# The opening of a relative-position attention: tokens of one batch normalised first, relative scores of two jobs in sets of four strips

## The chip, the cores and the metric

The kernel runs as one program on one core of a Trainium2 chip. The metric is the device time of one execution in microseconds (us), lower is better. Inside the core, TensorE (PE in the profile; its weight loads are PEld), VectorE (DVE), ScalarE (ACT), GpSimd (POOL) and the queue of SyncE (SP), which issues most DMAs, run side by side, each in its own written order, and meet only in semaphores.

## The reference

The model is four blocks on 4 batches of 512 tokens with 256 features: an attention with relative positions, an encoder layer with a mixture of experts, a cross attention, and a second mixture of experts. Only the beginning of the first block matters here. Cut to that:

```python
def _layernorm(x, axis=-1, eps=1e-05):
    m = jnp.mean(x, axis=axis, keepdims=True)
    v = jnp.var(x, axis=axis, keepdims=True)
    return (x - m) / jnp.sqrt(v + eps)
...
q = (jnp.einsum('bsd,ed->bse', query, Wq) + bq).reshape(B, S, H, dh).transpose(0, 2, 1, 3)
k = (jnp.einsum('bsd,ed->bse', key, Wk) + bk).reshape(B, S, H, dh).transpose(0, 2, 1, 3)
v = (jnp.einsum('bsd,ed->bse', value, Wv) + bv).reshape(B, S, H, dh).transpose(0, 2, 1, 3)
QEr = jnp.einsum('bhsd,ld->bhsl', q, Er_s)
Srel = _skew(QEr)
QK = jnp.einsum('bhsd,bhtd->bhst', q, k)
attn = (QK + Srel) / math.sqrt(dh)
attn = jnp.where(causal[None, None], attn, -jnp.inf)
attn = jax.nn.softmax(attn, axis=-1)
out = jnp.einsum('bhst,bhtd->bhsd', attn, v)
...
x = x + _L0_xattn_ref(_layernorm(x, axis=-1), ctx_1024, ctx_1024, ...)
```

The query is the normalised x, key and value are the context, there are 16 heads of 16 features, and everything is f32.

## The kernel before

**Tiles and jobs.** The 2048 tokens are 16 blocks of 128 (`TB`), four to a batch (`RT`). The first attention is done in 16 jobs (`NJ`), each four heads (`HQ`) of one batch. A job has eight units (`NUA`): row block r = 0 to 3 of the batch, and in each the pairs of heads pr = 0 and 1. Because of the causal mask row block r has 128(r+1) columns. A head occupies a strip of 32 partitions, so that four heads fill the 128 rows of the PE array. Two jobs share one projection of queries (`QPa`) or keys (`Ka`), and the zero-padded tables `ErP[0]` and `ErP[1]` pick which of the two jobs' heads a relative score is of.

**The relative scores** (QEr) make a trip through DRAM, which does the skew. `scores_a` on PE multiplies `QPa` by `ErP` into the two PSUM banks of `PD[0]`, `rel_copy` on ACT copies them to `EN[r]`, `rel_write` on SP writes `EN[r]` to DRAM once both pairs are in it, `rel_read` reads it back skewed into `SR[r]`, and GpSimd masks the diagonal (`rel_mask`). The relative scores run two jobs ahead of the key scores: in unit u of loop step n `scores_a(n, u)` issues the pair of relative scores of job n+2 and the pair of key scores of job n. The steps n = -2 and n = -1 are therefore the opening: they hold the relative scores of jobs 0 and 1 and no key scores, and between them the projections `queries_a`, `keys_a` and `values_to_bank_a`. A pair of relative scores may be issued only when ACT has copied the pair before, since there is one `PD[0]`. From n = 0 on DVE adds `SR` to the key scores and takes the row maximum (`row_max_a`), ACT takes the exponential, PE transposes, ACT and DVE copy the transposed weights to `PTa`, and PE multiplies them by the values.

**What stands ahead of the steps.** SP issues the loads in the order x (2 MB, whole), identity, constants, Wq, Wk, eight small pieces of Er, the context (2 MB), Wv, three rows. DVE waits for all of x, then takes the statistics of 16 blocks (`ln_part`, L1270 and L1273), ACT the square root (L1047), DVE normalises the 16 blocks into the four buffers of `nrm` (L1281), PE transposes them through two PSUM banks (`ln_transposes`, L604) and ACT copies them to `NT` (L1054). Only when all 16 are in `NT` does PE begin the first `queries_a`.

**The shared bank.** Queries, keys, values and outputs go through one PSUM bank `MB` in the order of the table `A_USES`; a use may be written only when the use before it has been read (`a_mr`).

Of the kernel before, what the change touches and what calls it, by code (L numbers as in the profile page):

```python
# [13 lines left out]
P = 128  # L14
D = 256
DK = D // P
# [55 lines left out]
A_USES = []  # L72
for _n in range(-3, NJ + 1):
    A_USES += [("k", (_n + 1) // 2)] * (_n % 2 == 1 and 0 <= _n + 1 < NJ)
    A_USES += [("q", 0)] * (_n == -3) + [("q", (_n + 4) // 2)] * (_n % 2 == 0 and _n + 4 < NJ)
    A_USES += [("v", _t) for _t in (range(RT) if _n == -1 else [_n + RT] * (0 <= _n < TB - RT))]
    A_USES += [("p", _n - 1), ("o", _n - 1)] * (_n >= 1)
# [40 lines left out]
def build(nc, A, out):  # L118

    with ExitStack() as ctx:  # L120
# [12 lines left out]
        def place(name, shape, dt, o=None):  # L133
            n = 1
            for s in shape[1:]:
# [137 lines left out]
              ("ctx0", "w0", "const", "x", "er", "wf", "wvo", "rows0", "late", "route", "ew", "w1", "ctx1", "rows1", "we0", "we")}  # L273
# [12 lines left out]
        for name, n in [("ln0", TB), ("ln1", TB), ("kvf", NJ // 2 + TB),  # L286
                        ("ont", TB), ("wo", TB), ("ln2", TB), ("rt0", 1), ("rank", 1), ("gt", 4), ("ln3", TB), ("ln4", TB), ("rt1", 1)]:
            USE[name], N_USE[name] = n_use, n
            n_use += n
# [36 lines left out]
        a_en = sem("a_rel_copied")  # L326
        a_w = [[sem(f"a_rel_written{i}_{r}") for r in range(RT)] for i in range(2)]
# [68 lines left out]
        def _(sp):  # L396
            sp.dma_start(X[:], A["x"].rearrange("(t p) d -> p t d", p=P)).then_inc(ld["x"], 16)
            sp.dma_start(idf[:], A["ident"]).then_inc(ld["const"], 16)
            sp.dma_start(cols[:], A["cols"]).then_inc(ld["const"], 16)
            for wa, w in ((WAq, "wq0T"), (WAk, "wk0T")):  # L400
                sp.dma_start(wa[:], A[w].rearrange("(k p) n -> p k n", p=P)).then_inc(ld["w0"], 16)
# [10 lines left out]
            def rel_write(n, r):  # L412
                sp.wait_ge(a_en, n * NUA + 2 * r + 2)
                if n >= 3:
                    sp.wait_ge(a_r[r], 16 * (n - 2))
                sp.dma_start(rel[n % 3][r], EN[r][:].rearrange("p h w -> p (h w)")).then_inc(a_w[n % 2][r], 16)
# [9 lines left out]
            for n in range(-2, NJ - 1):  # L426
                for r in range(RT):
                    if n + 2 < NJ:
                        rel_write(n + 2, r)
                    if n >= -1:  # L430
                        rel_read(n + 1, r)
# [158 lines left out]
        def _(pe):  # L590
# [17 lines left out]
            ln_transposes(0, "ln0", lambda tb: nrm[:, tb % 4])  # L608
            wait_all_stored(pe, "ln0")
            pe.wait_ge(ld["w0"], 32)  # L610
            pe.wait_ge(ld["er"], 32 * HQ)
            pe.wait_ge(ld["ctx0"], 32)

# [5 lines left out]
            def eight_heads(w, k, half):  # L619

                return w[:, k, half * P:half * P + P]

# [14 lines left out]
            def scores_a(n, u):  # L637
                r, pr = divmod(u, 2)
                w, e, ku = P * r + P, n + 2, n * NSU + 2 * u
                if e < NJ:  # L640
                    if u == 0:
                        pe.wait_ge(a_mr, A_AT["q", e // 2] + 1)
                    if e * NUA + u:
                        pe.wait_ge(a_en, e * NUA + u)
# [50 lines left out]

            queries_a(0)
            for n in range(-2, NJ + 1):
                for u in range(NUA):
# [11 lines left out]
                    if u == 2:  # L710
                        for tb in range(RT) if n == -1 else [n + RT] * (0 <= n < TB - RT):
                            values_to_bank_a(tb)
# [329 lines left out]
        def _(act):  # L1042
# [18 lines left out]
            ln_part(0, "ln0")  # L1061
            act.wait_ge(s_bp, 3)
# [13 lines left out]
            def rel_copy(n, u):  # L1076
                r, pr = divmod(u, 2)
                act.wait_ge(a_e, n * NUA + u + 1)
                if n and pr == 0:
                    act.wait_ge(a_w[(n - 1) % 2][r], 16 * ((n - 1) // 2 + 1))  # L1080
# [10 lines left out]
            def weights_a(t):  # L1091
                n, u = divmod(t, NUA)
                r, pr = divmod(u, 2)
                for i in range(A_UPTO[t - 1] if t else 0, A_UPTO[t]):
                    _, js, who, _ = A_GROUPS[i]
                    if who == "act":
                        act.wait_ge(a_tr, i + 1)
                        if n >= 2:
# [10 lines left out]

            queries_a(0)  # L1110
            for n in range(-2, NJ + 1):
                for u in range(NUA):
# [11 lines left out]
                    if 0 <= n < NJ:  # L1124
# [591 lines left out]
```

## Time and profile before

| | us |
|---|---|
| median of 3 runs | 2118.84 |
| lowest and highest | 2114.27, 2118.95 |
| the profiled execution | 2133.6 |
| its span, first to last instruction | 2131.9 |
| mean granted TensorE clock, share of full | 0.913 |
| busy PE, DVE, ACT, POOL | 1822.3, 1122.8, 843.2, 204.8 |
| before the first transpose on PE | 20.34 |
| from there to the first key score of job 0 | 65.51 |
| the 16 jobs of the first attention, up to the last transposes of outputs | 293 |

The stretch that the change touches is the first 86 us of the span. After it comes the loop over the jobs, and after that the other three blocks, which begin with a wait for everything that this attention adds to x. The granted clock is that of TensorE; a share of 1.00 is 2.4 GHz, 0.50 is 1.2 GHz. A row of a timeline gives start and length in us, engine, line, operation, output and input with their shapes and how many instructions are merged in it; in square brackets stands the idle time before it and what ended it. A matmul of f32 is counted twice in these rows, so "x4" is two matmuls.

### The profile page before, as it was taken

What the parts mean: (1) busy time and instruction counts of PE and PEld (TensorE: products, weight loads), DVE (VectorE), ACT (ScalarE), POOL (GpSimd) and SP (SyncE); (2) the same over time, 40 slices, a digit from 0 to 9 for tenths busy, and PEclk for the clock granted to TensorE, in tenths of its full rate; (3) what the DMA queues carried; (4) which work ended last, traced back from release to release, by engine and by line L of the source; (5) the groups of instructions that cost most, each with busy time, mean ns of one, the idle gap of its engine ahead of it and who ended that gap; (6) DMA issues with size and microseconds to landing.
All of it is one profiled execution on the core that took longest, in us unless ns stands there. A gap on an engine that the chain in (4) does not pass through costs nothing.

```text
span 2131.9 us, 31428 instructions
## 1 busy us (share of the span) xinstructions
PE 1822.3 (85%) x10594; PEld 1061.4 (50%) x10595; DVE 1122.8 (53%) x3014; ACT 843.2 (40%) x1951; POOL 204.8 (10%) x282
## 2 busy tenths in 40 slices
PE   4799999587777863999999089999999999977998
PEld 2355555242333452676676044445455445446886
DVE  2277777634555343222222466666666666655775
ACT  2488887414444330433333044544444444430000
POOL 0011111201111305000000520000000000020000
PEclk9799999677999955999999579999999999986999
DMA  4578886300000542111110600000000000020001
GB/s 137 199 276 292 283 293 213 119 0 1 1 1 1 182 138 86 32 32 32 34 32 25 212 1 1 1 1 1 1 1 1 1 1 1 1 79 0 0 0 40
DMA packets 63691, 146.68 MB, mean 69 GB/s; under 512 B 6345, under 2 KB 41297, under 8 KB 58961
## 3 DMA queue, kind: packets, MB, share of 16 engines
q1 hardware_dynamic: 60496, 136.69, 18.9%
q0 software_dynamic: 3072, 8.39, 1.2%
q8 instruction: 73, 1.20, 0.2%
q14 instruction: 50, 0.40, 0.1%
HBM read 86.34 MB, written 58.72 MB: 68 GB/s over the span
## 4 chain that ended last, share of the span: by engine, by line
PE 78%; DVE 7%; issue 7%; ACT 6%; POOL 2%; DMA 1%; SPq 0%; DVEq 0%; ACTq 0%; POOLq 0%
PE PS L596 11%; PE PS L1036 8%; PE PS L887 7%; PE PS L875 7%; PE PS L965 5%; PE PS L975 5%; PE PS L988 5%; PE PS L653 5%; PE PS L757 5%; PE PS L675 3%; PE PS L944 3%; PE PS L953 3%; PE PS L775 2%; PE PS L686 2%; PE PS L901 2%
## 5 line engine op out<-in xcount | busy, mean ns | idle before, releaser
L1224 ACT ACTIVATE P<-PS,nm 128x512 f32<-128x512 f32 x256 | 173.5, 682 | 317.2 <-DVE nm L1561 317.2
L1561 DVE TENSOR_REDUCE nm<-PS 128x2 f32<-128x1024 f32 x128 | 156.7, 1225 | 110.8 <-PE PS L965 110.7
L1383 DVE CUSTOM_DVE_ANT_0 dump<-PS,maskw 128x256 f32<-128x256 f32 (+3 forms) x256 | 115.4, 488 | 125.8 <-PE PS L762 117.7
L1321 DVE CUSTOM_DVE_ANT_0 SN<-PS,SR 128x128 f32<-128x128 f32 (+3 forms) x256 | 115.3, 488 | 91.1 <-PE PS L657 90.8
L975 PEld LDWEIGHTS PS<-idf,P 128*128 128x128 f32 x1024 | 109.6, 141 | 106.2 <-issue 105.5
L757 PE MATMUL PS<-QP,KP 32*128 32x256 f32 (+3 forms) x512 | 112.3, 518 | 57.2 <-DVE MX L1383 42.3
L887 PE MATMUL PS<-EW,xT 128*128 x320 | 147.1, 603 | 1.8 <-ACT xT L1187 1.3
L875 PE MATMUL PS<-EW,hT 128*128 x640 | 146.5, 383 | 2.4 <-ACT hT L1199 2.4
L975 PE MATMUL PS<-idf,P 128*128 128x128 f32 x1024 | 139.3, 279 | 8.2 <-ACT PTb L1233 8.2
L965 PE MATMUL PS<-K,Q 64*128 64x512 f32 x512 | 145.5, 645 | 0.9 <-DVE Q L1549 0.9
L653 PE MATMUL PS<-ErP,QPa 32*128 32x512 f32 (+3 forms) x512 | 114.0, 520 | 29.6 <-ACT EN L1082 20.6
L1652 DVE SCALAR_TENSOR_TENSOR X<-PS,gat,X 128x256 f32<-128x256 f32 x256 | 110.9, 479 | 53.1 <-PE PS L1036 51.9
L988 PE MATMUL PS<-PTb,V 128*64 128x512 f32 x512 | 137.4, 617 | 0.8 <-ACT O1T L1248 0.8
L1152 ACT ACTIVATE PTf<-PS 128x1024 f32<-128x1024 f32 (+3 forms) x128 | 89.5, 703 | 118.1 <-PE PS L757 118.0
L1199 ACT ACTIVATE hT<-PS,b1c 128x128 f32<-128x128 f32 x320 | 86.9, 383 | 122.9 <-PE PS L901 119.8
L604 PE MATMUL PS<-idf,nrm 128*128 128x128 f32 x128 | 40.1, 439 | 108.7 <-DVE nrm L1281 103.8
L1521 DVE COPY hS<-PS 128x512 f32<-128x512 f32 x80 | 55.3, 691 | 145.6 <-PE PS L887 145.6
L1089 ACT ACTIVATE SN<-SN,nm 128x128 f32<-128x128 f32 (+3 forms) x256 | 128.7, 555 | 6.0 <-DVE nm L1321 6.0
L875 PEld LDWEIGHTS PS<-EW,hT 128*128 128x128 f32 x640 | 119.7, 192 | 18.1 <-issue 3.1
L762 PE MATMUL PS<-KP,QP 32*128 32x384 f32 (+3 forms) x512 | 121.0, 550 | 7.6 <-DVE MX L1383 6.0
L1570 DVE TENSOR_SCALAR P<-P,rc 128x512 f32<-128x512 f32 x256 | 113.0, 484 | 4.6
L1082 ACT ACTIVATE EN<-PS 128x256 f32<-128x256 f32 (+3 forms) x128 | 89.7, 701 | 50.8 <-PE PS L653 50.6
(205 smaller groups left out, 3070.9 us busy)
## 6 DMA issues: line engine op xcount, KB each, us to landing
rel<-EN SPq DMA_DIRECT2D x16, 1024.0 KB, 4.8
SR<-rel SPq DMA_DIRECT2D x16, 1024.0 KB, 7.5
rel<-EN SPq DMA_DIRECT2D x16, 768.0 KB, 4.3
SR<-rel SPq DMA_DIRECT2D x16, 768.0 KB, 6.5
rel<-EN SPq DMA_DIRECT2D x16, 512.0 KB, 2.9
SR<-rel SPq DMA_DIRECT2D x16, 512.0 KB, 5.1
EW<-in_fc1T SPq DMA_DIRECT2D x8, 1024.0 KB, 12.0
EW<-in_fc2T SPq DMA_DIRECT2D x8, 1024.0 KB, 11.7
```

The lines of the kernel that those rows point to most:

```text
L596: last = mm(bank[0:m, 0:n], w(k), src(k), start=(k == 0), stop=(k == DK - 1))
L653: rel_mm = mm(PD[0][:, i, 0:w], QPa[e // 2 % 3][o:o + HQ8, r * P:r * P + P], ErP[e % 2][o:o + HQ8, S - w:S], start=True, stop=True)
L757: keys_mm = mm(PD[s % 2][:, x, 0:S - c * P], KP[o:o + HQ8, hg, b * S + c * P:b * S + c * P + P], QP[n % 4][o:o + HQ8, c * P:S], start=True ...
L875: last = mm(PS[5][:, 0:D], hT[:, f, :], EW[:, bass.ds(e, 1), o:o + D].rearrange("p e d -> p (e d)"), start=(f == 0), stop=(f == FK - 1))
L887: ins = mm(PS[1 + hf][:], xT[:, k, :], EW[:, bass.ds(e, 1), o:o + 512].rearrange("p e f -> p (e f)"), start=(k == 0), stop=(k == DK - 1))
L965: last = mm(PD[s % 2][:, j, :], Q1[m % 2][o:o + DH1, r * P:r * P + P], K1[m % 2][o:o + DH1, :], start=True, stop=True)
L975: last = nc.tensor.transpose(TR1[j][:, c * P:c * P + P], P1[s % 4][:, j, c * P:c * P + P], idf[:])
L988: last = mm(OUT1[o:o + DH1, :], V1[m % 2][:, c, o:o + DH1], PT1[m % 2][:, j, c, :], start=(c == 0), stop=(c == RT - 1), skip_group_check=True)
L1036: last = mm(PS[tb % 8][:], x[:, k, t], w[i][:, k, :], start=(n + k == 0), stop=(n + k == len(parts) + DK - 2))
L1089: af(sn, sn, ACT.Exp, bias=nm[:, (ku + i) % 16:(ku + i) % 16 + 1], scale=-1.0).then_inc(a_ex, 1)
L1224: last = af(P1[s % 4][:, j, :], PD[s % 2][:, j, :], ACT.Exp, bias=nm1[:, s % 4, j:j + 1], accum_out=sm1[:, s % 4, j:j + 1])
L1561: v.tensor_reduce(nm1[:, s % 4, :], PD[s % 2][:], AX.X, ALU.max, negate=True).then_inc(c_max, 1)
```

## The change

It rewrites the opening on all engines and leaves the loop from job 0 on nearly alone.

- **Loads.** x comes in two pieces, the 4 blocks of the first batch (512 KB) first, and the other 12 (1.5 MB) behind the context. Wk is issued behind Er, Wv behind the second piece of x.
- **Layer norm.** Statistics, square root and normalisation are done for blocks 0 to 3 first and for blocks 4 to 15 when their piece has come. The transposes go two blocks at a time through the shared bank `MB` (`tokens_a(i)`, uses `("l", i)`), with one ACT copy of 512 columns for two blocks: 0 and 1 ahead of the first queries, 2 and 3 ahead of the loop, 4 to 7 in units 3 to 6 of step n = 0.
- **Relative scores of jobs 0 and 1.** `rel_scores_a(n, r)` issues all four strips of a row block at once, into two of three bank pairs in turn (`PD[(2 * q + pr) % 3]`, q = 4n + r), and ACT and DVE copy one pair each (`rel_copy_first`), counted by `a_en` and by the new `a_end`. Job 1 is copied to `PTa[1]` in place of `EN`.
- **Order.** Queries 0, job 0, keys 0, queries 1, job 1, the values of the first batch, and then the loop from n = 0.

```diff
 A_USES = []
-for _n in range(-3, NJ + 1):
+A_USES = [("l", 0), ("l", 1), ("q", 0), ("k", 0), ("q", 1)] + [("v", _t) for _t in range(RT)] + [("l", 2), ("l", 3)]
+for _n in range(NJ + 1):
...
+    A_USES += [("l", _i) for _i in range(4, TB // 2)] * (_n == 0)
...
+            sp.dma_start(X[:, 0:RT], tokens[:, 0:RT]).then_inc(ld["x0"], 16)
...
+            sp.dma_start(WAk[:], A["wk0T"].rearrange("(k p) n -> p k n", p=P)).then_inc(ld["wk0"], 16)
             sp.dma_start(CTA[:], A["ctxT"].rearrange("(k p) t -> p k t", p=P)).then_inc(ld["ctx0"], 16)
-            sp.dma_start(WAv[:], A["wv0T"].rearrange("(k p) n -> p k n", p=P)).then_inc(ld["ctx0"], 16)
+            sp.dma_start(X[:, RT:], tokens[:, RT:]).then_inc(ld["x1"], 16)
...
+            def tokens_a(i):
+                bank_a(("l", i))
+                pe.wait_ge(ln_sem[0]["nrm"], 2 * i + 2)
+                for k in range(DK):
+                    for x in range(2):
+                        last = nc.tensor.transpose(MB[:, (2 * k + x) * P:(2 * k + x + 1) * P],
+                                                   nrm[:, (2 * i + x) % 4, k * P:k * P + P], idf[:])
+                last.then_inc(a_mw, 1)
+
+            def rel_scores_a(n, r):
+                w, q = P * r + P, n * RT + r
+                if q == 1:
+                    pe.wait_ge(a_en, q)
+                elif q >= 2:
+                    pe.wait_ge(a_en, q)
+                    pe.wait_ge(a_end, q - 1)
+                for pr in range(2):
+                    for i in range(2):
+                        o = HQ8 * (2 * pr + i)
+                        last = mm(PD[(2 * q + pr) % 3][:, i, 0:w], QPa[0][o:o + HQ8, r * P:r * P + P], ErP[n][o:o + HQ8, S - w:S],
+                                  start=True, stop=True)
+                last.then_inc(a_e, 1)
...
+                    if n == 0 and 3 <= u < 7:
+                        tokens_a(u + 1)
...
+            def rel_copy_first(n, r):
+                q, w = n * RT + r, P * r + P
+                act.wait_ge(a_e, q + 1)
+                to = PTa[1][r] if n else EN[r]
+                af(to[:, 0:2, :], PD[2 * q % 3][:, :, 0:w], ACT.Copy).then_inc(a_en, 1)
...
+            sqrt_a(0, 0, RT)
+            tokens_a(0)
+            tokens_a(1)
+            act.wait_ge(s_bp, 3)
             queries_a(0)
-            for n in range(-2, NJ + 1):
+            sqrt_a(1, RT, TB)
+            for r in range(RT):
+                rel_copy_first(0, r)
...
+            rstd_a(0, 0, RT)
+            normalise_a(0)
+            normalise_a(1)
+            dve.wait_ge(ld["x1"], 16)
+            stats_a(RT, TB)
+            for r in range(RT):
+                rel_copy_first(0, r)
```

How the instructions stand in three places, first before, then now. In these rows L is the line, then the operation, the output and after the arrow the inputs.

PE's opening before, from the transposes of all 16 blocks to the middle of job 1's relative scores (`ErP_89` is the table of even jobs, `ErP_90` that of odd ones, `QPa_61` the first queries):

```order
L604 MATMUL PS<-idf,nrm 128x128 x32
L596 MATMUL PS<-NT,WAq 128x512 x2
L653 MATMUL PS<-ErP_89,QPa_61 128x128 x4
L596 MATMUL PS<-NT,WAq 128x512 x2
L653 MATMUL PS<-ErP_89,QPa_61 128x256 x4
L653 MATMUL PS<-ErP_89,QPa_61 128x384 x4
L653 MATMUL PS<-ErP_89,QPa_61 128x512 x4
L653 MATMUL PS<-ErP_90,QPa_61 128x128 x2
L596 MATMUL PS<-CTA,WAk 128x512 x2
```

And now, up to the last transposes ahead of the loop:

```order
L637 MATMUL PS<-idf,nrm 128x128 x8
L611 MATMUL PS<-NT,WAq 128x512 x2
L651 MATMUL PS<-ErP_89,QPa_61 128x128 x4
L651 MATMUL PS<-ErP_89,QPa_61 128x256 x4
L651 MATMUL PS<-ErP_89,QPa_61 128x384 x4
L651 MATMUL PS<-ErP_89,QPa_61 128x512 x4
L611 MATMUL PS<-CTA,WAk 128x512 x2
L611 MATMUL PS<-NT,WAq 128x512 x2
L651 MATMUL PS<-ErP_90,QPa_61 128x128 x4
L651 MATMUL PS<-ErP_90,QPa_61 128x256 x4
L651 MATMUL PS<-ErP_90,QPa_61 128x384 x4
L651 MATMUL PS<-ErP_90,QPa_61 128x512 x4
```

Of the 32 transposes 8 are left at the head; the second queries stand behind the keys instead of inside job 0; the x4 of L653 were two issues of two matmuls with a wait between, those of L651 are one issue of four.

ACT's opening now, from the first square root to the copies of job 0 (before, one square root over all 16 blocks stood ahead of 32 copies to `NT`, and nothing but copies behind):

```order
L1115 ACTIVATE sd<-mv,eps_c 128x4
L1119 ACTIVATE NT<-PS 128x2x256 x2
L1129 ACTIVATE QPa_61<-PS,bq0s 128x512
L1115 ACTIVATE sd<-mv,eps_c 128x12
L1125 ACTIVATE EN_55<-PS 128x256
L1125 ACTIVATE EN_56<-PS 128x512
L1125 ACTIVATE EN_57<-PS 128x768
L1125 ACTIVATE EN_58<-PS 128x1024
```

The second square root, over the 12 later blocks, stands between the first queries and the first copy of a relative score. On DVE the 12 statistics stand in the same way ahead of its first copy.

ACT in step n = 0, units 3 to 5, now (before, the same rows without L1119):

```order
L1146 ACTIVATE EN_56<-PS 128x512
L1119 ACTIVATE NT<-PS 128x2x256
L1153 ACTIVATE SN_69<-SN_69,nm 128x256
L1153 ACTIVATE SN_70<-SN_70,nm 128x256
L1146 ACTIVATE EN_57<-PS 128x768
L1119 ACTIVATE NT<-PS 128x2x256
L1153 ACTIVATE SN_71<-SN_71,nm 128x384
L1153 ACTIVATE SN_72<-SN_72,nm 128x384
```

Between the copy of a relative score and the two exponentials of a unit there is now, in four units, a copy of 512 columns of transposed tokens.

## Rows read from the trace of the kernel before

**Rows 1.** Busy time by stretch: from:to, length, busy (x instructions), granted clock, DMA share, GB/s.

```profile
56.35:85.85 29.50, 21.68 (x53) 9.29 (x53) 1.70 (x4) 6.96 (x10) 1.51 (x3) 0.62 0.41 143
85.85:102.66 16.81, 14.61 (x96) 7.33 (x97) 10.29 (x38) 13.58 (x25) 2.29 (x4) 0.86 0.87 297
102.66:122.05 19.39, 17.52 (x196) 10.34 (x197) 13.31 (x47) 15.68 (x30) 1.90 (x3) 1.00 0.83 284
```

**Rows 2.** Timeline of PE in the opening: start, length, line, shapes, [idle before].

```profile
20.34 9.67 PE L604 MATMUL PS<-idf,nrm 128*128 128x128 f32 x32 [20.34 <-DVE nrm L1281]
30.59 3.75 PE L596 MATMUL PS<-NT,WAq 128*128 128x512 f32 x4 [0.58 <-ACT NT L1054]
35.18 0.80 PE L653 MATMUL PS<-ErP,QPa 32*128 32x128 f32 x4 [0.84 <-ACT QPa L1066]
36.46 0.80 PE L653 MATMUL PS<-ErP,QPa 32*128 32x128 f32 x4 [0.48 <-ACT EN L1082]
...
42.82 1.22 PE L653 MATMUL PS<-ErP,QPa 32*128 32x256 f32 x4 [0.70 <-ACT EN L1082]
44.74 1.65 PE L653 MATMUL PS<-ErP,QPa 32*128 32x384 f32 x4 [0.70 <-ACT EN L1082]
47.30 1.65 PE L653 MATMUL PS<-ErP,QPa 32*128 32x384 f32 x4 [0.91 <-ACT EN L1082]
49.86 2.08 PE L653 MATMUL PS<-ErP,QPa 32*128 32x512 f32 x4 [0.91 <-ACT EN L1082]
53.06 2.08 PE L653 MATMUL PS<-ErP,QPa 32*128 32x512 f32 x4 [1.12 <-ACT EN L1082]
...
57.08 3.28 PE L596 MATMUL PS<-CTA,WAk 128*128 128x512 f32 x4
...
70.35 2.08 PE L596 MATMUL PS<-WAv,CTA 128*128 128x256 f32 x4 [0.52 <-DVE VE L1308]
...
85.85 0.55 PE L653 MATMUL PS<-ErP,QPa 32*128 32x128 f32 x1 [1.17 <-issue]
```

**Rows 3.** Timeline of ACT, opening and step n = 0, same columns.

```profile
19.15 0.31 ACT L1047 ACTIVATE sd<-mv,eps_c 128x16 f32<-128x16 f32 x1
...
34.44 0.69 ACT L1066 ACTIVATE QPa<-PS,bq0s 128x512 f32<-128x512 f32 x1 [3.95 <-PE PS L596]
...
60.40 1.44 ACT L1072 ACTIVATE Ka<-PS,bpad,hmask 128x512 f32<-128x512 f32 x2 [2.83 <-PE PS L596]
...
95.38 0.81 ACT L1082 ACTIVATE EN<-PS 128x768 f32<-128x768 f32 x1 [0.21 <-PE PS L653]
96.08 1.11 ACT L1089 ACTIVATE SN<-SN,nm 128x384 f32<-128x384 f32 x2
```

**Rows 4.** Timeline of DVE, statistics of the layer norm.

```profile
11.25 5.32 DVE L1270 BATCH_NORM_STATS2 st<-X 128x6 f32<-128x256 f32 x16
16.60 1.17 DVE L1273 BATCH_NORM_AGGREGATE mv<-st 128x2 f32<-128x6 f32 x16
```

**Rows 5.** DMA from 0 to 60 us: GB/s in 40 slices of 1.5 us; issues with KB and us to landing.

```profile
GB/s 0 133 327 359 368 338 343 223 373 426 415 349 137 23 0 0 0 0 0 0 0 0 0 0 0 116 59 0 0 0 276 74 0 123 401 0 0 0 426 268
...
X<-in_x SPq DMA_DIRECT2D x1, 2048.0 KB, 9.0
CTA<-in_ctxT SPq DMA_DIRECT2D x1, 2048.0 KB, 8.3
```

**Rows 6.** Timeline of SP's queue: the second issue, and that of the context.

```profile
1.32 2.23 SPq L398 DMA_DIRECT2D idf<-in_ident  x1
...
9.52 0.42 SPq L407 DMA_DIRECT2D CTA<-in_ctxT  x1
```

**Rows 7.** L657 on PE: a pair alone (timeline), a pair beside L653's (stretch).

```profile
367.68 1.13 PE L657 MATMUL PS<-Ka,QPa 32*128 32x512 f32 x4
...
336.50:337.80 1.30, 1.13 (x4) 0.31 (x4) 1.00 0.75 287
```

**Rows 8.** Timeline of PE in step n = 0: four transposes.

```profile
97.10 0.66 PE L675 MATMUL PS<-idf,SN 128*128 128x128 f32 x4
```

More of the change, by code:

```diff
@@ L424, in rel_read @@
                 sp.dma_start(SR[r][:].rearrange("p h w -> p (h w)"), skewed).then_inc(a_r[r], 16)
-            for n in range(-2, NJ - 1):
+            for r in range(RT):
+                rel_write(0, r)
+                if r:
+                    rel_read(0, r - 1)
+            rel_read(0, RT - 1)
+            for r in range(RT):
+                rel_write(1, r)
+            for n in range(NJ - 1):
                 for r in range(RT):
@@ L607, in _ @@
             pe.wait_ge(ld["const"], 32)
[L608 to L612, printed above, removed]
             def bank_a(use):
@@ L694, in out_to_tokens_a @@
                 last.then_inc(a_mw, 1)
+            tokens_a(0)
+            tokens_a(1)
+            pe.wait_ge(ld["w0"], 16)
             queries_a(0)
-            for n in range(-2, NJ + 1):
+            pe.wait_ge(ld["er"], 32 * HQ)
+            pe.wait_ge(a_mr, A_AT["q", 0] + 1)
+            for r in range(RT):
+                rel_scores_a(0, r)
+            pe.wait_ge(ld["wk0"], 16)
+            pe.wait_ge(ld["ctx0"], 16)
+            keys_a(0)
+            queries_a(1)
+            for r in range(RT):
+                rel_scores_a(1, r)
+            pe.wait_ge(ld["wv0"], 16)
+            for tb in range(RT):
+                values_to_bank_a(tb)
+            tokens_a(2)
+            tokens_a(3)
+            for n in range(NJ + 1):
                 for u in range(NUA):
@@ L709, in _ @@
                         queries_a((n + 4) // 2)
[L710 to L712 removed]
+                    if u == 2 and n < TB - RT:
+                        values_to_bank_a(n + RT)
+                    if n == 0 and 3 <= u < 7:
+                        tokens_a(u + 1)
                     if u == 7 and n >= 1:
@@ L1108, in copy_out_a @@
                 af(OSa[n % 2][:], MB[:], ACT.Copy).then_inc(a_mr, 1)
+            sqrt_a(0, 0, RT)
+            tokens_a(0)
+            tokens_a(1)
+            act.wait_ge(s_bp, 3)
             queries_a(0)
-            for n in range(-2, NJ + 1):
+            sqrt_a(1, RT, TB)
+            for r in range(RT):
+                rel_copy_first(0, r)
+            keys_a(0)
+            queries_a(1)
+            for r in range(RT):
+                rel_copy_first(1, r)
+            tokens_a(2)
+            tokens_a(3)
+            for n in range(NJ + 1):
                 for u in range(NUA):
@@ L1347, in outputs_a @@
                                 rc.unsqueeze(3).to_broadcast([P, RT, HQ, DH0]), ALU.mult).then_inc(a_mr, 1)
-            for n in range(-2, NJ + 2):
+            for tb in range(RT):
+                values_a(tb)
+            normalise_a(4)
+            normalise_a(5)
+            for n in range(NJ + 2):
                 for u in range(NUA):
@@ L1357, in _ @@
                         weights_a(t)
-                    if u == 2:
-                        for tb in range(RT) if n == -1 else [n + RT] * (0 <= n < TB - RT):
-                            values_a(tb)
+                    if u == 2 and n < TB - RT:
+                        values_a(n + RT)
+                    if n == 0 and u in (4, 5):
+                        normalise_a(u + 2)
             dve.wait_ge(a_x, NJ)
```

93 lines of the change are left out of this document (68 added, 25 removed).

## The prediction, made before the changed kernel ran

> **What bounds the kernel now.** I read first the busy times by stretch, then the timelines of PE, ACT and DVE over the first 100 us, then the DMA rates and the queue of SP. In the loop over the jobs PE is busy for 17.52 of 19.39 us [rows 1]; the opening is unlike it. Up to 20.34 us PE has nothing to do, and what it waits for is DVE, which takes statistics of all 16 blocks once all of x is there [rows 2, 4]. From 35.18 us on PE and ACT take turns: PE issues one pair of relative scores, waits for ACT's copy, issues the next [rows 2]. Nobody is saturated there; the time is the sum of a chain. Its pitch, from one start to the next, is 1.28 us for 128 columns (35.18 to 36.46), 1.92 for 256 (42.82 to 44.74), 2.56 for 384 (44.74 to 47.30) and 3.20 for 512 (49.86 to 53.06) [rows 2]. PE also runs at its lower level: a pair of 512 columns takes 2.08 us here and 1.13 us later at granted clock 1.00 [rows 2, 7], and the stretch up to the loop shows 0.62 granted [rows 1]. The loop with job 0 begins at 85.85 us [rows 2]. Everything behind it is a chain on it, so what the opening gives is given at the end. (A change of about 0.3%, 6.4 us, is what a measurement here can tell from none.)
>
> **The change part by part,** as a new clock for the beginning.
>
> *The first batch alone.* In the kernel before, 9 us pass between the start of the statistics and the first transpose. With 4 blocks these take a quarter of 5.32 and 1.17 us, so PE starts at about 9 us and at the latest near 14, if the first piece of x came no earlier than all of x did (9.8 us, from the landing) [rows 4, 5]. Two sets of four transposes at the 1.2 us that eight such sets took in 9.67 us, each with a copy of about 0.84 us with its handoffs, and the queries at 3.75 us put the end of the first queries at 17 to 22 us [rows 2]. The next part shows that this start hardly counts.
>
> *A new wait.* ACT takes its second square root ahead of the first copy of relative scores, and that needs the statistics of blocks 4 to 15, which need the second piece of x. Queued behind it on ACT are all copies of job 0, and PE's second row block waits for the first of them; on DVE the 12 statistics stand ahead of its own copies too. So the landing of the second piece sets the chain. The context took 8.3 us from an issue at 9.52 us [rows 5, 6]. Its issue now comes at the same place in the queue; the identity's issue took 2.23 us behind the large x [rows 6], which I expect to shrink by up to 1.5 us behind a quarter of it, so the context is issued at 8.0 to 9.5. Its 2.1 MB need 5.1 us at about 415 GB/s with some 3 us around them, and lands at 16.0 to 17.5; the second piece, 1.57 MB at the 327 to 368 GB/s at which x moved, needs 4.6 us more: 20.6 to 22.1, I take 21.4 [rows 5]. The Trainium skill (DMA: Bandwidth & Descriptors, Anatomy of one DMA) gives for a DMA 2.0 us plus its bytes at 436 GB/s, though fitted on GpSimd's queue. By that x would have taken 6.8 us where the trace has 9.0, and the second piece would land near 18.4, which would add 3 us to the gain.
>
> Then 12 statistics, three quarters of 5.32 and of 1.17 us, are 4.87 us [rows 4], the square root 0.31 with 0.08 ahead [rows 3]: ACT is free at 26.7. PE, which finished row block 0 long before, waits here for some 8 us.
>
> *Four strips at once.* Does a set of four cost twice a pair? In the loop a pair of key scores with 512 columns takes 1.13 us alone, and 1.13 us too where a pair of relative scores is issued beside it [rows 7]. So four cost what two did. ACT still copies one pair per set, and DVE copies the other at the same time and may be one set late. The pitch per set stays that of a pair, and there are 8 sets where there were 16. From 26.7: ACT's copy of set 0 and handoff 0.48 (1.28 less 0.80), then 1.92, 2.56 and the last 2.08 on PE: 33.7 [rows 2]. No row shows ACT and DVE copying from PSUM side by side. The bound above is that each copy takes as long as two: pitch less PE's part is 0.48, 0.70, 0.91 and 1.12 us, so 3.2 us more for a job and 6.4 for both; below it is nothing, since nothing is taken from ACT's copies. I take none, as the pitches contain one copy of the same size each.
>
> *Keys and queries 1* stand in a row now, both through the shared bank: 3.75, copies of 1.44 with 0.1, 3.75, and the copy 0.84 [rows 2, 3]: 43.6. *Job 1:* 0.45 for its first copy, 1.92, 2.56 and 2.08: 50.6. *Values:* four times 2.60 (2.08 and 0.52 idle) [rows 2]: 61.0. *Blocks 4 to 7:* two sets of 1.2 with one 0.84 between: 64.3. There the loop begins, against 85.85: **21.6 us earlier**. The trip of job 0 through DRAM is no limit: its last write can be issued at about 35 us and the reads follow at once, nearly 30 us before DVE wants them.
>
> *What moves into the loop.* Four sets of transposes and four copies of 512 columns in units 3 to 6 of n = 0. That stretch is ACT's: copy 0.81 and exponentials 1.11 us, with 0.21 idle [rows 3]. Each copy adds 0.69 less the overlap of neighbours, some 0.6, and the first one waits about 0.5 for its transposes (0.66 us on PE [rows 8]): 3.0 us. Bounds: 2.4 (nothing waits) to 4.9 (each copy waits for PE as the first does). The six normalisations that DVE makes beside are covered: it is busy 10.29 of 16.81 us there [rows 1]; without this cover they would be some 2 us.
>
> *The clock.* My sum has the lower level throughout the opening. In the kernel before, the keys took 3.28 instead of 3.75 us [rows 2], so the level rose for a moment behind an unbroken run of PE. Now the keys follow directly on the last set of job 0, 5.8 us of PE without a gap, and the second queries on little. I take 1.4 us for a rise that comes once more and a little longer than before; the ends are 0 and the 8 us of the rival below.
>
> **Sum:** 21.6 - 3.0 + 1.4 = 20.0 us. The profiled execution would go from 2133.6 to 2113.6, and the median from 2118.84 to **2098.8 us**.
>
> **The rivals.** *A: the clock goes up in the opening and stays.* From 33.7 to 64.3 PE works some 22 us of 30.6 at the lower level; at the higher for three quarters of that, 8 us go: a gain of about 27, 2092 us. For it speaks the denser run, against it that in the values, 2.08 of 2.60 us busy, the level fell and stayed low before. *B: the copies in n = 0 wait each time,* or ACT and DVE hinder each other: 3 to 6 us less, a gain of 15, 2104 us. *C: slower.* In the kernel before, the stretch from 85.85 to 102.66 has 0.86 granted [rows 1], which is a rise to the full level near 90.5 us; now it fails to rise as early, since tokens' transposes and longer waits for ACT now thin out PE's work there. A job holds 17.52 us of PE at full clock [rows 1]; at half it is some 16 us longer. One and a third jobs at the lower level eat the whole gain, two make it 12 us slower: 2131 us. Against it: the second queries' like, `queries_a(2)`, stands in unit 1 of n = 0 as before, right before the rise. The Trainium skill (TensorE: Matmul & The Clock Gate, Part 4) says that transposes don't count as activity for that clock. By it the eight transposes ahead of the loop would leave PE at the lower level at its start, which is where the kernel before was too. *D: it does not do what it says.* If the second piece of x came only with the last rows, beyond 30 us, or the new waits set ACT, DVE and PE in a circle of turns that is as long as before, the gain would be below 6 us: 2113 or more. Nothing in the queue of SP, a single one that was served in order, speaks for it.
>
> **How the numbers follow.** Forecast (gain 16 to 24) 0.60; A 0.16; B 0.15; between them and the page's earlier landing 0.03; C 0.03; D 0.03. The range takes in A and B with the bounds of the landing: 2091 to 2107 us, about 0.85. Faster by over 0.3%: 0.94; within 0.3%: 0.03; slower: 0.03.
>
> **What would show it.** PE's first transposes at 9 us (14 at most); a gap on PE of some 8 us behind the first set of relative scores, ended by ACT, whose square root of 12 columns ends at 26.7; sets of 512 columns at 2.08 us with eight instructions, pitches as before; the loop's first scores at 63 to 64.5 us; step n = 0 of about 20 us against 16.81. I am wrong if that gap is missing (x lands early, more gain), if sets of four take longer than 2.1 us, if the copies run long beside each other, or if the clock's share differs in the stretch from 34 to 64 us or in the first job.

## The result, and the profile after

| | before | after |
|---|---|---|
| median of the runs, side by side | 2118.89 us (2114.27 to 2120.01) | 2091.66 us (2090.76 to 2092.22) |
| ratio | | 0.9853, 95% interval 0.9817 to 0.989 |
| profiled execution, its span | 2133.6, 2131.9 us | 2092.2, 2090.5 us |
| loop with job 0 begins | 85.85 us | 53.61 us |

Faster, and by more than the 20.0 us forecast: the ratio stands for 31 us (23 to 39), the two medians lie 27.2 us apart, and the medians of all runs of the two kernels in this study (39 of before, 10 of after) 28.6 us. 2091.66 us is where the first rival had put the time (2092), at the lower edge of the stated range of 2091 to 2107.

PE in the opening of the changed kernel, the view of [rows 2] (start, length, line, shapes, idle before):

```profile
9.46 1.09 PE L637 MATMUL PS<-idf,nrm 128*128 128x128 f32 x4 [9.46 <-DVE nrm L1390]
...
17.82 0.81 PE L651 MATMUL PS<-ErP,QPa 32*128 32x128 f32 x8 [0.93 <-ACT QPa L1129]
25.31 1.24 PE L651 MATMUL PS<-ErP,QPa 32*128 32x256 f32 x8 [6.68 <-ACT EN L1125]
27.27 1.66 PE L651 MATMUL PS<-ErP,QPa 32*128 32x384 f32 x8 [0.72 <-ACT EN L1125]
29.86 2.09 PE L651 MATMUL PS<-ErP,QPa 32*128 32x512 f32 x8 [0.93 <-ACT EN L1125]
31.88 3.78 PE L611 MATMUL PS<-CTA,WAk 128*128 128x512 f32 x4
37.20 1.98 PE L611 MATMUL PS<-NT,WAq 128*128 128x512 f32 x4 [1.54 <-ACT Ka L1135]
39.11 0.50 PE L651 MATMUL PS<-ErP,QPa 32*128 32x128 f32 x8
40.23 0.71 PE L651 MATMUL PS<-ErP,QPa 32*128 32x256 f32 x8 [0.62 <-ACT PTa L1125]
...
43.52 1.14 PE L651 MATMUL PS<-ErP,QPa 32*128 32x512 f32 x8 [0.93 <-ACT PTa L1125]
44.59 1.13 PE L611 MATMUL PS<-WAv,CTA 128*128 128x256 f32 x4
...
50.03 1.13 PE L611 MATMUL PS<-WAv,CTA 128*128 128x256 f32 x4 [0.52 <-DVE VE L1426]
51.68 0.66 PE L637 MATMUL PS<-idf,nrm 128*128 128x128 f32 x4 [0.52 <-DVE VE L1426]
```

Read the second column down a shape. The two projections of 512 columns (L611) take 3.78 us at 31.88 and 1.98 at 37.20; a set of four strips of 512 columns takes 2.09 us in job 0 and 1.14 in job 1; values take 1.13 us where they took 2.08 before [rows 2]. By these lengths TensorE runs at 1.2 GHz up to about 36 us and at 2.4 GHz from there to the loop. The chain is the one forecast, turn for turn. Its gap stands at the foreseen place, 6.68 us ended by ACT. What that gap waits for, on ACT and DVE (same columns):

```profile
24.69 0.30 ACT L1115 ACTIVATE sd<-mv,eps_c 128x12 f32<-128x12 f32 x1 [7.01 <-DVE mv L1379]
...
32.02 1.02 ACT L1125 ACTIVATE EN<-PS 128x1024 f32<-128x1024 f32 x1 [2.21 <-PE PS L651]
```

```profile
19.69 4.02 DVE L1376 BATCH_NORM_STATS2 st<-X 128x6 f32<-128x256 f32 x12 [9.73 <-DMA X<-in_x]
...
32.02 1.23 DVE L1397 COPY EN<-PS 128x1024 f32<-128x1024 f32 x1 [2.06 <-PE PS L651]
```

The copy that PE waits for stands behind a square root over statistics that nobody needs yet, and these behind the second piece of x. The last rows show ACT and DVE each copying 1024 columns out of PSUM from 32.02 us on, side by side.

Busy time by stretch, columns as in [rows 1]: the first 35 us, step n = 0, the 18 us ahead of the loop, and the encoder's attention (441 to 678 us).

```profile
0.00:35.00 35.00, 14.81 (x48) 5.89 (x49) 14.59 (x54) 6.47 (x10) 1.85 (x8) 1.00 0.72 235
53.61:70.22 16.61, 14.45 (x113) 8.18 (x113) 12.85 (x46) 15.78 (x30) 1.27 (x2) 1.00 0.56 186
36.00:53.61 17.61, 10.89 (x60) 5.48 (x60) 5.73 (x10) 5.14 (x8) 1.34 (x3) 1.00 0.76 281
441.00:677.80 236.80, 180.12 (x1604) 75.22 (x1604) 124.50 (x511) 107.56 (x156) 39.59 (x63) 0.92 0.00 1
```

The granted clock ahead of the loop is 1.00 where it was 0.62 [rows 1]. But the column reads 1.00 in the first 35 us too, where every known shape takes its long time (3.78 us for keys or queries, 2.09 for a set of 512 columns), so in the opening I go by these lengths and not by the column. The last row has a partner in the kernel before that explains why the two spans differ by 41.4 us and the runs by less. There the same stage, with the same work, reads:

```profile
473.40:718.50 245.10, 188.37 (x1602) 76.43 (x1604) 124.52 (x511) 107.38 (x156) 39.49 (x63) 0.89 0.00 1
```

It is 8.3 us longer at 0.89 granted against 0.92, hundreds of microseconds behind the edit. Across the profiles of this study that stage is between 229.3 and 245.1 us long, with both kernels at different places in it (before 245.1 and 239.0, after 236.8 and 234.2). So I judge each experiment by the start of the loop in its profile, and by its runs only to some 5 us. From the first key score of the loop to its last 285.2 us pass before and 284.7 after, and what follows outside the encoder's stage agrees to 1 us (102.3 and 102.7; 1413.4 and 1412.7).

### The profile page after: what moved, and what is told of

Same layout as the page of the kernel before. It is cut to its first block, busy times and chain, and to the rows that moved or that the text cites. A ratio compares the mean times of both kernels' runs of the same rounds, so it can differ in the third digit from the quotient of the medians.

```text
span 2090.5 us, 31424 instructions
## 1 busy us (share of the span) xinstructions
PE 1791.5 (86%) x10594; PEld 1052.6 (50%) x10595; DVE 1128.9 (54%) x3023; ACT 835.7 (40%) x1920; POOL 205.5 (10%) x282
## 4 chain that ended last, share of the span: by engine, by line
PE 78%; DVE 7%; ACT 6%; issue 4%; POOL 3%; DMA 1%; SPq 0%; DVEq 0%; POOLq 0%; ACTq 0%
PE PS L611 11%; PE PS L1088 8%; PE PS L939 7%; PE PS L927 7%; PE PS L1017 5%; PE PS L1027 5%; PE PS L1040 5%; PE PS L809 5%; PE PS L686 4%; PE PS L708 3%; PE PS L996 3%; PE PS L1005 3%; PE PS L827 2%; PE PS L719 2%; PE PS L953 2%
## 5 line engine op out<-in xcount | busy, mean ns | idle before, releaser
L619 PE MATMUL PS<-idf,nrm 128*128 128x128 f32 x96 | 31.3, 442 | 88.0 <-DVE nrm L1362 83.9
L686 PE MATMUL PS<-ErP,QPa 32*128 32x128 f32 (+3 forms) x448 | 91.2, 479 | 16.5 <-ACT EN L1146 8.8
L690 PE MATMUL PS<-Ka,QPa 32*128 32x512 f32 (+3 forms) x512 | 104.3, 480 | 0.8 <-DVE nm L1439 0.6
```

The source lines that it names most:

```text
L686: rel_mm = mm(PD[0][:, i, 0:w], QPa[e // 2 % 3][o:o + HQ8, r * P:r * P + P], ErP[e % 2][o:o + HQ8, S - w:S], start=True, stop=True)
```

## The experiments

The theory formed on seeing the rows above: the 32 us come from the early start and, for the larger part, from the four strips with the clock that they bring. Against it stood that the early start alone brought the clock, and, of the clock, that it needs an unbroken run of PE, as in the keys directly behind job 0.

**The four strips without the early start.** All of x is loaded and normalised first, as before; everything else is as in the changed kernel.

```diff
-            sp.dma_start(X[:, 0:RT], tokens[:, 0:RT]).then_inc(ld["x0"], 16)
+            sp.dma_start(X[:], tokens).then_inc(ld["x0"], 16)
...
-            sqrt_a(0, 0, RT)
-            tokens_a(0)
-            tokens_a(1)
+            sqrt_a(0, 0, TB)
+            for i in range(TB // 2):
+                tokens_a(i)
...
-            sqrt_a(1, RT, TB)
...
-                    if n == 0 and 3 <= u < 7:
-                        tokens_a(u + 1)
```

> The changed kernel with the loading and the layer norm as before it (all of x first, statistics of 16 blocks, eight sets of transposes ahead of the first queries, none in the loop); the four strips at once stay. Theory (the parts add, and the clock rises behind keys and queries wherever they stand): eight sets at 1.9 us from 20.3 put the first queries near 35.5, job 0 near 40 to 48, and the loop starts near 67.5 instead of 53.6, while step n = 0 is 2.5 to 3 us shorter: 11 us slower than the changed kernel, about 2103. Rival (most of the gain is the early start, four strips are worth little): 2108 or more.

Measured: 2100.08 us (2095.24 to 2100.68), ratio to before 0.9893 (0.9866 to 0.9921), loop at 62.80 us: 9.2 us later than with the early start, 23.0 earlier than before. That was 4.7 us earlier than expected. The first queries stood at 33.29 for 35.5, as DVE takes the statistics from 9.41 us on where they began at 11.25 [rows 4] (in the kernel before it first waited for the constants), and in job 0 and the keys the clock was better than assumed. PE:

```profile
33.29 3.57 PE L609 MATMUL PS<-NT,WAq 128*128 128x512 f32 x4 [0.78 <-ACT NT L1113]
...
38.78 0.71 PE L649 MATMUL PS<-ErP,QPa 32*128 32x256 f32 x8 [0.49 <-ACT EN L1119]
40.21 1.66 PE L649 MATMUL PS<-ErP,QPa 32*128 32x384 f32 x8 [0.72 <-ACT EN L1119]
42.80 2.09 PE L649 MATMUL PS<-ErP,QPa 32*128 32x512 f32 x8 [0.93 <-ACT EN L1119]
44.83 2.93 PE L609 MATMUL PS<-CTA,WAk 128*128 128x512 f32 x4
```

The level rises, falls again in the turns of job 0 (0.71 us for 256 columns, then 1.66 for 384) and rises for good in the keys. So the clock doesn't come from the early start. And since the first queries come 2.7 us later here than in the kernel before (33.29 against 30.59 [rows 2], through one shared bank), the order of the work behind them with the four strips gives rather more than 23.0 us. The same kernel prices what moved into the loop. Its step n = 0, without the four sets of transposes, at 1.00 granted as well:

```profile
62.80:77.80 15.00, 12.78 (x100) 6.44 (x99) 10.74 (x39) 13.61 (x25) 1.27 (x2) 1.00 0.60 198
```

15.00 us against 16.61: the move costs 1.6 us, and ACT's busy time grows by 2.17.

**The early start without the four strips.** Job 0 and job 1 issue a pair at a time and ACT copies all.

```diff
-                if q == 1:
-                    pe.wait_ge(a_en, q)
-                elif q >= 2:
-                    pe.wait_ge(a_en, q)
-                    pe.wait_ge(a_end, q - 1)
                 for pr in range(2):
+                    if 2 * q + pr:
+                        pe.wait_ge(a_pn, 2 * q + pr)
                     for i in range(2):
...
-                last.then_inc(a_e, 1)
+                    last.then_inc(a_p, 1)
```

> The changed kernel with the relative scores of jobs 0 and 1 in pairs again, one bank pair, ACT copying all of them; everything else stays. Theory: job 0 costs 9 us more (pitches 1.28, 1.92, 2.56 and 3.20 twice), job 1 6.5 us more at the full clock level (pitches 1.12, 1.44, 1.85 and 2.07): 15.5 us, about 2107. Rival (the clock's rise near 36 us was owed to the dense run that four strips make; with pairs it comes later or not): the loop starts 20 us or more later, 2112 to 2115.

Measured: 2114.26 us (2110.51 to 2118.37), ratio 0.9969 (0.9949 to 0.9989), loop at 76.9 us, 23.3 later than in the changed kernel. The rival held. Job 0 lasts 23.2 us to the keys (17.76 to 40.98) where it was 14.1 (17.82 to 31.88), almost all of it at the low level in both, so some 9 us are the price of turns alone. From job 1 to the loop it is 29.0 us against 14.5. The expectation had priced 6.5 of these 14.5 us for turns at the full level; by that estimate the other 8 are the clock's. PE in job 1 and the values:

```profile
45.99 1.98 PE L611 MATMUL PS<-NT,WAq 128*128 128x512 f32 x4 [1.54 <-ACT Ka L1134]
...
50.00 0.70 PE L648 MATMUL PS<-ErP,QPa 32*128 32x256 f32 x4 [0.48 <-ACT PTa L1124]
51.39 1.22 PE L648 MATMUL PS<-ErP,QPa 32*128 32x256 f32 x4 [0.70 <-ACT PTa L1124]
...
63.64 2.08 PE L611 MATMUL PS<-WAv,CTA 128*128 128x256 f32 x4
66.30 2.07 PE L611 MATMUL PS<-WAv,CTA 128*128 128x256 f32 x4 [0.59 <-DVE VE L1415]
```

```profile
51.00:76.90 25.90, 19.04 (x44) 8.64 (x44) 2.43 (x6) 5.21 (x7) 0.64 (x1) 0.50 0.25 102
```

The level rises in the keys here too, and is lost at the second pair of 256 columns; the stretch from 51 us to the loop has 0.50 granted. The values here and in the changed kernel are the same instructions, with the same 0.52 us for DVE between the later ones. Behind pairs that had lost the level they take 2.08 us each and stay there; behind four quick sets they take 1.13 and stay there, even past a first pause of 1.01 us. PE is the busier in the first case (2.08 of 2.60 us, against 1.13 of 1.65), and that doesn't lift it.

To reach them at the full level is not enough, though. In the kernel before, the pair ahead of the values was quick and the first values matmuls were already slowing down, before any pause of their own:

```profile
62.17 0.70 PE L653 MATMUL PS<-ErP,QPa 32*128 32x256 f32 x4 [1.39 <-ACT EN L1082]
62.80 1.78 PE L596 MATMUL PS<-WAv,CTA 128*128 128x256 f32 x4
```

The next three take 2.07 and 2.08 us [rows 2], and the second profile of that kernel shows the same (0.70 at 61.14, then 1.47 and 2.08). There the turns ahead were thin: 0.49 us of work, 1.39 idle, 0.70 of work. So in these kernels the level in the values went with what stood ahead of them, not with their own busy share and not with the level at their first instruction alone. It wasn't chance either: all nine profiles with quick sets in job 1 keep the level through the values, and the three with pairs have all but the first at 2.07 or 2.08 us.

What each of the two edits gives adds up: 85.85 to 76.9 is 8.9 us (the early start with all else but the strips), and 85.85 to 62.80 is 23.0, together 32.0 of the 32.2 measured.

The Trainium skill (TensorE: Matmul & The Clock Gate, A second HAM failure mode: psum-queue depth-cycling) describes such a kernel, whose PE goes idle for a moment between groups of matmuls and so swings between the two levels. The pairs of job 1 show the fall (0.70 us busy, 0.70 idle, then 1.22 for the same shape) and no way back up; the values at 1.13 and 0.52 idle don't show it.

**Is an unbroken run needed?** PE waits for ACT's last copy of job 0 ahead of the keys.

```diff
             pe.wait_ge(ld["ctx0"], 16)
+            pe.wait_ge(a_en, RT)
             keys_a(0)
```

> The changed kernel with one wait more: PE starts the keys only when ACT has copied the last set of job 0, so that PE's run through the last set and the keys is broken by the copy's 1.1 us. Theory (the clock's rise behind that run is what the forecast lacked): without the unbroken run the level rises later, with the second queries or in job 1, and the loop starts 1.1 plus 1 to 4 us later: 2094 to 2097. Rival (keys and queries are enough by themselves): only the 1.1 us, 2092.8.

Measured: 2097.19 us (2087.35 to 2100.67), ratio 0.9884 (0.9856 to 0.9912), loop at 55.8 us.

```profile
34.38 3.47 PE L611 MATMUL PS<-CTA,WAk 128*128 128x512 f32 x4 [1.34 <-ACT EN L1126]
39.39 1.98 PE L611 MATMUL PS<-NT,WAq 128*128 128x512 f32 x4 [1.54 <-ACT Ka L1136]
```

My theory fell: with 1.34 us of idle ahead of the keys the level rises all the same, and inside them. An unbroken run from the last set into the keys isn't what it needs. The loop begins only 2.2 us later, of which 1.1 is the second set starting later (26.40 against 25.31) because x landed later. The median is 5 to 7 us above the changed kernel's, and these 2.2 us don't explain that; its profile has the encoder's stage at 242.1 us, whose cause I don't know.

**Can idle PE time be filled to raise the clock early?** Three, then six, matmuls whose result nobody reads, in the gap behind the first set.

```diff
                 rel_scores_a(0, r)
+                if r == 0:
+                    for _ in range(3):
+                        mm(PS[5][:], NT[:, 0, 0:P], NT[:, 0, 0:S], start=True, stop=True)
```

> The changed kernel with three f32 matmuls of 128x512 whose result nobody reads, into an idle bank, in PE's gap behind the first set of relative scores. Theory (the level follows PE's work just before): the level has risen by 25 us; sets 2 to 4 of job 0 and the keys run at the full level, 0.5, 0.7, 0.95 and 1.85 us shorter: 4 us less, about 2087.7. Rival (the rise near 36 us comes for another reason): the sets keep 1.24, 1.66 and 2.09 us, the time stays at 2091.7.

> As with three fillers, but with six f32 matmuls of 128x512 in PE's gap behind the first set of job 0. With three, the level was full through the fillers (2.84 us for three) and had fallen after 4.2 us without work, when set 2 came at 25.0. Theory (idleness lets it fall): six end within 2 us of set 2, so sets 2 to 4 and the keys run at the full level, 0.5, 0.7, 0.95 us and about 1 us less: the loop starts near 50 instead of 52.3, about 2087; where the first queries leave the level low, six fillers take up to 11 us instead of 5.7 and the time is up to 3 us longer than with three. Rival (the level does not depend on the gap): sets at 1.24, 1.66 and 2.09 as before, 2089 to 2092.

Measured with three: 2089.31 us (2086.22 to 2093.24), ratio 0.985 (0.9822 to 0.9879), loop at 52.3.

```profile
17.95 2.84 PE L739 MATMUL PS<-NT 128*128 128x512 f32 x6
25.00 1.23 PE L651 MATMUL PS<-ErP,QPa 32*128 32x256 f32 x8 [4.21 <-ACT EN L1128]
```

Measured with six: 2089.87 us (2085.27 to 2091.14), ratio 0.9854 (0.983 to 0.9879), loop at 49.8.

```profile
18.56 6.96 PE L739 MATMUL PS<-NT 128*128 128x512 f32 x12
25.45 0.71 PE L651 MATMUL PS<-ErP,QPa 32*128 32x256 f32 x8
26.88 0.93 PE L651 MATMUL PS<-ErP,QPa 32*128 32x384 f32 x8 [0.72 <-ACT EN L1128]
...
29.81 1.98 PE L611 MATMUL PS<-CTA,WAk 128*128 128x512 f32 x4
```

Three end 4.21 us before the second set, and by then the level is low again (1.23 us), as that run's rival had it. (The first set took 0.50 us even ahead of the fillers: in most of the later profiles the level had risen by the end of the first queries and fell in the gap behind the first set.) Six leave no idle time; job 0 and the keys run at the full level, and the loop begins 3.8 us earlier than at 53.61. In the median, 2 us at most, it can't be told from the changed kernel.

**Who should wait for the second piece of x?** First the later statistics and their square root go behind what job 0 needs (ACT: behind the second queries; DVE: behind its copies). Then, instead, that piece is loaded ahead of the context.

```diff
             queries_a(0)
-            sqrt_a(1, RT, TB)
             for r in range(RT):
                 rel_copy_first(0, r)
             keys_a(0)
             queries_a(1)
+            sqrt_a(1, RT, TB)
...
-            dve.wait_ge(ld["x1"], 16)
-            stats_a(RT, TB)
             for r in range(RT):
                 rel_copy_first(0, r)
+            dve.wait_ge(ld["x1"], 16)
+            stats_a(RT, TB)
```

> The changed kernel with the statistics of blocks 4 to 15 on DVE behind the copies of job 0, and the second square root on ACT behind the second queries, so that no copy waits for the second piece of x. Theory: PE's gap of 6.7 us behind the first set goes, all else follows: the loop starts near 47, about 2085. Rival (the gap is given back: keys wait for the context, or the clock level rises later in the run than the work now comes, so that keys and queries run at the lower level): 2088 to 2092.

```diff
-            sp.dma_start(CTA[:], A["ctxT"].rearrange("(k p) t -> p k t", p=P)).then_inc(ld["ctx0"], 16)
             sp.dma_start(X[:, RT:], tokens[:, RT:]).then_inc(ld["x1"], 16)
+            sp.dma_start(CTA[:], A["ctxT"].rearrange("(k p) t -> p k t", p=P)).then_inc(ld["ctx0"], 16)
```

> The changed kernel with the second piece of x issued ahead of the context, nothing else moved. Theory (ACT and DVE hold all of PE for that piece): it lands near 15, statistics end near 20, set 2 starts near 20.5 instead of 25.3, the context lands near 19.5 and is in time for the keys at 27: the loop starts 4.8 us earlier, 2087. Rival (the context becomes the wait that ends last, or the level falls otherwise): 2090 to 2092.

Measured: 2086.71 us (2080.17 to 2089.58) at 0.9828 (0.9798 to 0.9858), loop at 46.3; and 2086.85 us (2083.07 to 2096.46) at 0.9854 (0.9823 to 0.9885), loop at 46.9. PE with the late statistics, at the place of the 6.68 us:

```profile
17.72 0.50 PE L651 MATMUL PS<-ErP,QPa 32*128 32x128 f32 x8 [0.93 <-ACT QPa L1129]
18.72 0.71 PE L651 MATMUL PS<-ErP,QPa 32*128 32x256 f32 x8 [0.49 <-ACT EN L1125]
```

The gap is 0.49 us; with the other order of the loads it is 1.78. Both confirm that the added wait held the chain, and price it at 7.3 us, 6.7 with the order of the loads, at the loop's start. That price isn't the wait alone. With the late statistics 6.2 us are the gap; the first two sets at the full level and keys that reach it sooner (3.00 us for 3.78) give some 1.7, and 0.6 goes back in job 1, where PE waits for DVE (1.12 us ahead of the third set). The runs say less: the medians are 4 to 5 us below the changed kernel's, but the two ratios are 0.9828 and 0.9854 against its 0.9853 and 0.9856, that is 5 to 6 us less for the late statistics and nothing for the order of the loads.

**The best of both.** The late statistics, and five matmuls on zeros in the first 9 us, when PE has nothing to do.

```diff
+            nc.gpsimd.memset(SN[0][:], 0.0).then_inc(s_zw, 1)
...
+            pe.wait_ge(s_zw, 1)
+            for _ in range(5):
+                mm(PS[5][:], SN[0][:, 0:P], SN[0][:], start=True, stop=True)
             pe.wait_ge(ld["const"], 32)
```

> The kernel with the late statistics, and PE given five f32 matmuls of 128x512 on zeros from 2.5 us on, while it waits for the first tokens; nobody reads them. Theory (the level follows PE's work, whatever the data): the first transposes, queries, sets 3 and 4 and the keys run at the full level, 0.5, 0.5, 1.8, 1.7 and 1.1 us less: the loop starts near 41 instead of 46.3, about 2081. Rival (zeros or matmuls outside a dense run do not lift it, or it falls again before 9.4 us): 2086.7.

Measured: 2078.34 us (2076.40 to 2085.20), ratio 0.9812 (0.9787 to 0.9838), loop at 42.7: faster than both kernels.

```profile
2.35 6.54 PE L626 MATMUL PS<-SN 128*128 128x512 f32 x10 [2.35 <-POOL SN L537]
9.50 0.63 PE L642 MATMUL PS<-idf,nrm 128*128 128x128 f32 x4 [0.61 <-DVE nrm L1395]
...
12.25 1.96 PE L613 MATMUL PS<-NT,WAq 128*128 128x512 f32 x4 [0.78 <-ACT NT L1124]
...
19.42 1.56 PE L656 MATMUL PS<-ErP,QPa 32*128 32x512 f32 x8 [0.93 <-ACT EN L1130]
20.91 3.22 PE L613 MATMUL PS<-CTA,WAk 128*128 128x512 f32 x4
```

The first transposes and queries run at the full level; it is lost in the last set of job 0 (1.56 where 1.14 is the full time) and comes back in the keys. The loop begins 3.6 us earlier than with the late statistics alone. The medians differ by 8.4 us, but the kernel before, run beside each of the two, had 2123.87 us with the late statistics and 2119.36 here. By the ratios (0.9828 and 0.9812) the step is some 3 us, which agrees with the opening.

**Both kernels once more,** unchanged, for the scatter of the clock.

> The changed kernel, unaltered. The question is what of the 32.8 us by which its first attention ended earlier the whole time keeps. Theory (everything behind the first attention is the same chain, apart from the length of the encoder's attention, which was 229, 237 or 245 us in the traces so far, whatever the kernel): the loop starts near 53.6 again, ends near 338, and the time is 2084 to 2100 with the encoder's stage taking one of these lengths. Rival (the gain is partly given back behind the loop): the loop starts near 53.6 and the stages behind it are longer than before by 5 us with the encoder's length unchanged.

> The kernel before, unaltered, for a second trace of the same program. Theory (the opening's chain is fixed, the encoder's stage is not): the loop starts within 2 us of 85.9, its length is 285 to 288, and the encoder's stage has 229, 237 or 245 us, where it had 245. Rival (245 us belongs to this kernel): 245 again.

Measured: 2090.44 us (2086.00 to 2102.48) for the changed kernel, ratio 0.9856 (0.9818 to 0.9894), loop at 53.0; one run of 2125.86 us for the one before, loop at 84.5. PE of the latter:

```profile
42.73 0.70 PE L653 MATMUL PS<-ErP,QPa 32*128 32x256 f32 x4 [0.70 <-ACT EN L1082]
44.13 0.91 PE L653 MATMUL PS<-ErP,QPa 32*128 32x384 f32 x4 [0.70 <-ACT EN L1082]
45.95 1.65 PE L653 MATMUL PS<-ErP,QPa 32*128 32x384 f32 x4 [0.91 <-ACT EN L1082]
```

The level moves about between executions of one kernel: here it was up for two pairs where [rows 2] has none. It was lost within two turns again, and the start of the loop moves by 1.4 us.

## Why the prediction was right and wrong

*The start.* First transposes forecast at 9 us, measured at 9.46.

*The landing of the second piece of x.* Said 21.4 (20.6 to 22.1), measured 19.65, where the context takes 8.1 us (8.3 before) and the piece then 4.5 us at the forecast rate. The issue was mis-sized. SP's queue (the view of [rows 6]):

```profile
1.32 0.49 SPq L401 DMA_DIRECT2D idf<-in_ident  x1
...
7.02 0.47 SPq L410 DMA_DIRECT2D CTA<-in_ctxT  x1
...
8.04 4.99 SPq L412 DMA_DIRECT2D WAv<-in_wv0T  x1
```

The identity's issue fell from 2.23 to 0.49 us and the context's came at 7.02 where I had 8.0 to 9.5. That gives 1.8 us. By the Trainium skill (DMA: Bandwidth & Descriptors, Anatomy of one DMA; 2.0 us plus the bytes at 436 GB/s, fitted on GpSimd's queue) the context would take an estimated 6.8 us; the trace has 8.1, so the row was the better guide.

*The new wait.* Right: 6.68 us for "some 8", ended by ACT, whose square root ended at 24.99 for 26.7. Moving the statistics took the gap away.

*Four strips cost what two did, and ACT and DVE don't hinder each other.* Right: 1.14 us against 1.13, 2.09 against 2.08; pitches from 25.31 on of 1.96 and 2.59 us for 1.92 and 2.56. None of the 3.2 us bounded for hindering showed.

*The chain up to the keys.* Keys forecast at 33.7, measured at 31.88: the landing's 1.8 us and no more.

*The clock: the step that failed.* I took 1.4 us, from ends of 0 and 8. The loop's start came 10.7 us ahead of the forecast 64.3; less the landing's 1.8, some 8.9 us are left for the clock. Piece by piece it is the same: the four values alone take 7.1 us to the next transposes (44.59 to 51.68) for the 10.4 forecast, job 1 up to the values 5.5 for 7.8, the queries 1.98 for 3.75, and the last transposes up to the loop 1.9 for 3.3: 8.8 us. The rival had the mechanism and, at 8 us, nearly the size; that its total of 27 us then met the runs' median is partly luck, since it left out the landing and the loop's smaller price and the encoder's stage scatters by more than they are worth. I held against it that in the kernel before "in the values, 2.08 of 2.60 us busy, the level fell and stayed low". The level there fell in the first of the values (1.78 us), ahead of their pauses, behind thin turns of pairs. The row showed only that such work doesn't lift the level, and I read it as showing that such work can't keep it. And I left the chance of the rise at the keys, which the kernel before shows (3.28 for 3.75), without asking what would follow it: before, slow turns of pairs that lose the level again; now, four quick sets and then the values. That job 1 loses it in pairs and keeps it in sets of four, behind the same keys and queries, is shown by the second experiment. It is no rule for sets of four: in job 0 of the first one, and with the late statistics, they lost it at the third set (1.66 us). By what measure of the engine's work, stays open.

*What moved into the loop.* Said 3.0 (2.4 to 4.9; by its own terms, four waits of 0.5 on top of 2.4, the upper bound is 4.4), measured 1.6. The copies took 0.60 us as said, but lay partly in what had been ACT's idle time, and the first of them waited 0.19 us for its transposes where I had 0.5; the normalisations stayed covered. The whole loop is 284.7 us with the move and 283.4 without, 1.3 us.

*The sum.* 21.6 plus 1.8 for the landing and 8.8 for the clock, piece by piece, is 32.2, as measured; the loop's 1.6 us of added work are more than offset by what step n = 0 no longer loses to the clock (0.86 granted before, now 1.00; 16.81 us against 16.61), so 32.7 us are left where the first attention ends (379.14 before, 346.41 after). The runs give 27 to 31, with an interval that holds this number.

*The slower rival.* It asked whether the level fails to rise in step n = 0. The level was there before the loop began. But six of the nine profiles with sets of four lost it at the loop's start, right behind the last transposes of tokens, among them the changed kernel's second one (queries at 54.66 of 3.51 us for 1.98). It was back within those queries or right behind them, so this costs some 1.5 us, not a job's 16. The three that kept it are the changed kernel's first profile, the one with six fillers, and the one with no transposes there (63 us in the first experiment).

## What to carry to other kernels

Where several engines take turns, each turn's fixed part is paid per turn, so halving the number of turns pays twice: once in the turns, and once more if the denser work keeps TensorE's clock. Price a stretch at both levels, and look at what stands ahead of it; its own busy share didn't tell here which level it would have (80% at the low one, 69% at the full one). When work is started on a part of the data, look at what is queued ahead of it on each engine for the rest of the data: here one square root in the wrong place cost 7 us at the start of the loop, of 40 that could be had.

## What the runs showed of the hardware

- The clock of TensorE in a stretch depended on what ran ahead of it: the values stayed at 2.08 us (0.52 idle between) behind slow pairs and at 1.13 us (0.52 idle) behind quick sets, same code; reached at the full level behind thin turns (0.49 busy, 1.39 idle, 0.70 busy) they lost it in the first one (1.78 us). It rose in the keys or right behind them in all profiles but that with six fillers, where it was up already; with 1.34 us of idle ahead of them too, and elsewhere on matmuls whose result is discarded, on zeros too.
- It fell in turns of half busy, half idle (0.70 and 0.70 us in pairs, 0.71 and 0.72 in job 0's sets of four), and in a gap of 4.21 us; a gap of 1.78 us left it (0.50 us ahead for 128 columns, 0.71 behind for 256).
- The granted clock read 1.00 for the first 35 us of the changed kernel, in which every shape took the time of the low level.
- One stage of 1,600 matmuls, hundreds of microseconds behind every edit, took from 229.3 to 245.1 us, with 0.95 to 0.89 granted. Here is its shortest, in the profile with the pairs, with the same ACT and DVE times as the longest above:

```profile
467.10:696.40 229.30, 172.61 (x1604) 74.00 (x1604) 124.54 (x511) 107.55 (x156) 39.72 (x63) 0.95 0.00 1
```

- Copies of 1024 columns from PSUM by ACT and DVE at the same moment took 1.02 and 1.23 us (ACT alone, in the kernel before: 1.02); the smaller ones (0.36 and 0.60 on ACT) kept the pitch of pairs copied alone.
- SP's issue of a small transfer took 0.49 us behind 512 KB of x and 2.23 behind 2048 KB, and one behind the context and the second piece of x 4.99, but one behind the context alone, in the kernel before, 0.47 (at 9.98). The same issue can cost ten times as much by its place; by what rule, these runs don't show.
